# Attention in a hybrid block: exps over two score banks, accumulator copied one step later, maxima split on POOL, rotation from PSUM, first half head by four banks

## The reference, cut to what matters

```
q, k, v = x @ Wq + bq, x @ Wk + bk, x @ Wv + bv      # 16 heads of width 16
q, k = rope(q), rope(k)       # x1*cos - x2*sin, x1*sin + x2*cos
scores = q @ k.T / sqrt(16)   # 4096 x 4096 per head
out = softmax(scores) @ v @ Wo + bo
```

## Time and profile before

| what | value |
|---|---|
| median of 3 runs | 3953.17 us (3945.92 to 3953.18) |
| profiled execution | 3957.6 us, its span 3955.0 us |
| granted clock of PE over the span | 0.953 |
| PE busy | 3614.0 us (91%) |
| DVE busy | 3493.7 us (88%) |
| ACT busy | 2576.7 us (65%) |
| POOL busy | 624.6 us (16%) |
| rotation stage | about 741 to 875 us |
| waiting for the first head's rows | 879.6 to 911.3 us |
| first half head, maxima alone | 912 to 988.6 us |
| steps of attention | about 1001 to 3819 us |
| after attention | 3820 us to the end |

### The profile page before, as it was taken

One profiled execution on the slowest core, in us unless ns is written; L12 is line 12 of the kernel. 1 busy time (PEld: TensorE's weight loads), 2 busy tenths in 40 slices (PEclk: granted clock), 3 DMA queues, 4 the chain that ended last, 5 costly groups with the idle time before them and its releaser, 6 DMA issues. The chain is left out here.

```text
span 3955.0 us, 68507 instructions
## 1 busy us (share of the span) xinstructions
PE 3614.0 (91%) x18757; PEld 1001.7 (25%) x18784; DVE 3493.7 (88%) x5278; ACT 2576.7 (65%) x4673; POOL 624.6 (16%) x436
## 2 busy tenths in 40 slices
PE   5788888857999999999999999999999999999988
PEld 2122222421222222222222222222222222222234
DVE  5999997777999998999999999999999998999815
ACT  5444443550677777777777777777777777777764
POOL 2789894370000000000000000000000000000020
PEclk9899999975899999999999999999999999999999
DMA  1000000341100101010001101000100100010011
GB/s 58 0 1 1 0 0 0 88 99 17 25 13 18 27 3 27 3 27 3 28 12 19 27 3 27 3 27 3 27 19 12 27 3 27 3 27 3 3 53 43
DMA packets 49365, 79.44 MB, mean 20 GB/s; under 512 B 12400, under 2 KB 39536, under 8 KB 44912
## 3 DMA queue, kind: packets, MB, share of 16 engines
q1 hardware_dynamic: 48496, 73.99, 8.2%
q10 hardware_dynamic: 512, 1.05, 0.2%
HBM read 53.37 MB, written 21.23 MB: 19 GB/s over the span
## 5 line engine op out<-in xcount | busy, mean ns | idle before, releaser
L1285 DVE TENSOR_REDUCE part_max<-max_scores 128x1 f32<-128x512 f32 x4096 | 2629.8, 686 | 202.2 <-PE max_scores L1166 154.2
L1267 ACT ACTIVATE prob<-scores 128x512 f32<-128x512 f32 x4096 | 2108.6, 604 | 700.0 <-PE scores L1202 700.0
L1202 PE MATMUL scores<-q_rows,k_rows 99*128 99x512 bf16 x4096 | 1095.6, 387 | 37.2 <-ACT prob L1267 28.4
L1214 PE MATMUL acc<-prob,v_ones 128*32 128x512 f32 x8192 | 1112.7, 616 | 0.0
L1163 PE MATMUL max_scores<-k_twin,q_twin 64*128 64x512 bf16 x2048 | 817.8, 400 | 72.6 <-DMA k_twin<-qk_parts 54.7
L1166 PE MATMUL max_scores<-k_rows,q_rows 64*128 64x512 bf16 x2048 | 818.3, 400 | 20.6 <-DVE part_max L1285 19.6
L1163 PEld LDWEIGHTS max_scores<-k_twin,q_twin 64*128 64x128 bf16 x2048 | 190.1, 93 | 1371.0 <-DVE part_max L1285 1268.1
L1202 PEld LDWEIGHTS scores<-q_rows,k_rows 99*128 99x128 bf16 x4096 | 321.9, 98 | 575.8 <-ACT prob L1267 308.8
L1139 POOL COPY v_ones<-v_all 128x512 f32 (+1 forms) x16 | 9.7, 612 | 2600.6 <-PE acc L1214 2600.5
L512 ACT ACTIVATE decay<-delta,a_scale 128x1024 f32<-128x1024 f32 (+1 forms) x128 | 143.1, 1118 | 300.2 <-DVE scan_state L559 300.2
L597 POOL TENSOR_TENSOR scan_hc<-scan_state,c_rep 128x1024 f32<-128x1024 f32 x128 | 301.8, 2358 | 0.7 <-issue 0.6
(11 more groups left out here) (119 smaller groups left out, 1393.1 us busy)
## 6 DMA issues: line engine op xcount, KB each, us to landing
qk_parts<-roped_parts SPq DMA_DIRECT2D x64, 192.0 KB, 2.9
q_rows<-qk_parts SPq DMA_DIRECT2D x192, 64.0 KB
k_rows<-qk_parts SPq DMA_DIRECT2D x180, 64.0 KB
q_twin<-qk_parts SPq DMA_DIRECT2D x128, 64.0 KB
x_res<-in_x SPq DMA_DIRECT2D x4, 1024.0 KB, 8.8
rope_trig<-in_trig SPq DMA_DIRECT2D x4, 1024.0 KB, 9.0
att_t<-acc_sb SPq DMA_DIRECT2D x128, 32.0 KB
att_all<-att_t SPq DMA_DIRECT2D x8, 512.0 KB, 7.6
```

The costliest lines, as they stand in the source:

```text
L1202: nc.tensor.matmul(sc[:, n % SB, :], k_rows[0:KM, par, kt * P:(kt + 1) * P], q_rows[0:KM, par, q0:q0 + CH], start=True, stop=True).then_in ...
L1214: last = nc.tensor.matmul(acc[32 * i:32 * i + VW, :], v_ones[:, par, kt, :], prob[:, t % PBUF, i * CH:(i + 1) * CH], start=(kt == 0), stop ...
L1267: nc.scalar.activation(prob[:, t % PBUF, j * CH:(j + 1) * CH], sc[:, n % SB, :], ACT.Exp, scale=SCALE).then_inc(exp_done, 1)
L1285: nc.vector.tensor_reduce(part_max[:, t, c:c + 1], mx[:, unit_bank(h, half, u), :], AXX, ALU.max).then_inc(max_read, 1)
```

## The change

Five edits, all in the attention part:

1. One exp instruction covers two score banks (1024 columns) instead of one, so there are two per step. It waits for both score matmuls, and sets both banks free at its end.
2. `acc` is copied behind the exps of the step after (`t == 1` and `t == NKT + 1`).
3. DVE only reduces the maxima to one per query; the four operations that cut it into parts stand on POOL. The partial maxima have a buffer per half head.
4. The rotation multiplies with the sine first, straight from PSUM, and ACT then copies the product crosswise (SBUF to SBUF); the cosine term is written back to PSUM in place; DVE adds the two. The sum leaves POOL, and the low part moves from DVE to POOL. PE may write a bank again once the sum is formed (`roped_ready`).
5. The first half head uses all eight PSUM banks: four max units go to four banks, and one DVE reduction covers the 2048 columns. `qk_parts` is laid out so that a DMA fetches 16 rows instead of 8 (20 DMAs per head), and the first max unit awaits only 16 DMAs: the rows that it uses, and of q only the first half of the queries. The rest is awaited before the second half head's units.

```diff
-        sc = ctx.enter_context(nc.psum_tensor("scores", [P, SB, CH], F32))
-        acc = ctx.enter_context(nc.psum_tensor("acc", [P, CH], F32))
-        mx = ctx.enter_context(nc.psum_tensor("max_scores", [P, MB, CH], F32))
+        banks = ctx.enter_context(nc.psum_tensor("att_banks", [P, 8, CH], F32))
+        sc, acc, mx = banks[:, 0:SB, :], banks[:, SB, :], banks[:, SB + 1:SB + 1 + MB, :]
...
@@ attention, scalar
-                        for j in range(4):
+                        for j in range(0, 4, 2):
                             n = 4 * t + j
-                            act.wait_ge(s_ready, h * (4 * STEPS) + n + 1)
-                            nc.scalar.activation(prob[:, t % PBUF, j * CH:(j + 1) * CH], sc[:, n % SB, :], ACT.Exp,
-                                                 scale=SCALE).then_inc(exp_done, 1)
-                        if t == 0 and not first:
+                            act.wait_ge(s_ready, h * (4 * STEPS) + n + 2)
+                            nc.scalar.activation(prob[:, t % PBUF, j * CH:(j + 2) * CH].rearrange(
+                                "p (b q) -> p b q", q=CH), sc[:, n % SB:n % SB + 2, :], ACT.Exp,
+                                                 scale=SCALE).then_inc(exp_done, 2)
+                        if t == 1 and not first:
                             copy_block(h - 1, 1)
-                        if t == NKT:
+                        if t == NKT + 1:
                             copy_block(h, 0)
...
@@ attention, gpsimd
+                def split_max(h, half):
+
+                    b, cols = 2 * h + half, slice(half * QT, (half + 1) * QT)
+                    wait_apart(pool, low_ready, b + 1, pool_passed)
+                    nc.gpsimd.tensor_copy(neg_parts[:, 0, cols], neg_max[:]).then_inc(split_step, 1)
+                    wait_apart(pool, split_step, b * 3 + 1, pool_passed)
+                    nc.gpsimd.tensor_tensor(neg_rest[:], neg_max[:], neg_parts[:, 0, cols],
+                                            ALU.subtract).then_inc(split_step, 1)
...
                     for par in range(2):
+                        split_max(2 * pair + par, 1)
+                        split_max(2 * pair + par + 1, 0)
 
                         pool.wait_ge(pv_done, (2 * pair + par + 1) * STEPS)
                         copy_v(2 * pair + 2 + par, par)
...
@@ attention, loads and first half head
-                for s in range(2):
-                    r = base + n * DK + s * DK // 2
-                    eng.dma_start(rows[r:r + DK // 2, par, :],
-                                  mem.qk_parts[which, part, s, bass.ds(h * (DK // 2), DK // 2), :]
-                                  ).then_inc(rows_loaded, 16)
+                if n >= skip:
+                    r = base + n * DK
+                    eng.dma_start(rows[r:r + DK, par, cols],
+                                  mem.qk_parts[which, part, bass.ds(h * (DK // 2), DK // 2), :, cols].rearrange(
+                                      "r s t -> (r s) t")).then_inc(done, 16)
...
+                pe.wait_ge(first_loaded, FIRST_LOAD)
                 for u in range(MAXU):
-                    max_unit(0, 0, 0, u)
+                    t, c, g = u // NC, u % NC, u // WIDE
+                    q, out = slice(t * P, (t + 1) * P), wide_banks(g)[:, u % WIDE, :]
+                    if u % WIDE == 0 and g >= 2:
+                        pe.wait_ge(first_read, g - 1)
...
+                pe.wait_ge(rest_loaded, REST_LOAD)
+                pe.wait_ge(first_read, MAXU // WIDE)
...
+                for g in range(MAXU // WIDE):
+                    dve.wait_ge(first_ready, (g + 1) * WIDE)
+                    t, m = g // (NC // WIDE), g % (NC // WIDE)
+                    nc.vector.tensor_reduce(part_max[:, 0, t, m:m + 1], wide_banks(g), mybir.AxisListType.XY,
+                                            ALU.max).then_inc(first_read, 1)
...
@@ attention_project, vector
+                    dve.wait_ge(qk_ready, g + 1)
+                    if later(g - NU + 1):
+                        dve.wait_ge(swap_ready, g - NU + 1)
+                    nc.vector.scalar_tensor_tensor(cross[:, n], qb[:, n], b_qk[:, a, h:h + 1],
+                                                   trig[:, 1, bass.ts(i, CH)], ALU.add, ALU.mult).then_inc(cross_ready, 1)
+                    nc.vector.scalar_tensor_tensor(qb[:, n], qb[:, n], b_qk[:, a, h:h + 1],
+                                                   trig[:, 0, bass.ts(i, CH)], ALU.add, ALU.mult).then_inc(own_ready, 1)
+
+                def add_cross(g, n):
+
+                    dve.wait_ge(own_ready, g + 1)
+                    dve.wait_ge(swap_ready, g + 1)
+                    if later(g - NU + 1):
+                        dve.wait_ge(rest_ready, g - NU + 1)
+                    nc.vector.tensor_tensor(roped[:, n], qb[:, n], swapped[:, n], ALU.add).then_inc(roped_ready, 1)
```

More of the change, by code:

```diff
@@ L801, in attention_project @@
         (loaded, trig_here, std_ready, rstd_ready, xn_ready, t_ready, xnt_ready, v_ready, v_read, qk_ready,
-         swap_ready, terms, roped_ready, hi_ready, rest_ready, mid_ready, lo_ready, stats_done) = make_sems(
-            nc, ctx, "ap", "loaded trighere std rstd xn t xnt v vread qk swap terms roped hi rest mid lo stats")
+         cross_ready, swap_ready, own_ready, roped_ready, hi_ready, rest_ready, mid_ready, lo_ready, stats_done) = make_sems(
+            nc, ctx, "ap", "loaded trighere std rstd xn t xnt v vread qk cross swap own roped hi rest mid lo stats")
         stored = make_sems(nc, ctx, "ap", "stored0 stored1 stored2 stored3")
@@ L864, in pair @@
                                 copy_turned(i + 1, 1 - b)
-                            act.wait_ge(qk_ready, g + 1)
-                            if later(g - NU + 1):
-                                act.wait_ge(terms, g - NU + 1)
-                            nc.scalar.activation(swapped[0:HP, n], qb[HP:P, n], ACT.Copy)
-                            nc.scalar.activation(swapped[HP:P, n], qb[0:HP, n], ACT.Copy).then_inc(swap_ready, 1)
+                            swap(g, n)
                             if later(g):
@@ L890, in what_hi_leaves, with low @@
                                             ALU.subtract).then_inc(rest_ready, 1)
+                def low(g, n):
+                    pool.wait_ge(mid_ready, g + 1)
+                    nc.gpsimd.tensor_tensor(parts[:, n, 2], rest[:, n], parts[:, n, 1],
+                                            ALU.subtract).then_inc(lo_ready, 1)
                 def chunk(i, first, last_chunk):
@@ L894, in chunk @@
                         g = i * NU + n
[L896 to L900 removed]
+                        what_hi_leaves(g, n)
                         if later(g):
[L902 removed]
+                            low(g - 1, (n - 1) % NU)
                 ends_apart(pool, NC, chunk)
[L905 removed]
+                low(NC * NU - 1, NU - 1)
             @block.vector
@@ L958, in _ @@
                 ends_apart(dve, NC // 2, pair)
-                low(NC * NU - 2, NU - 2)
-                low(NC * NU - 1, NU - 1)
+                add_cross(NC * NU - 1, NU - 1)
             @block.tensor
@@ L1050, in turned, with load_rows, load_even_blocks @@
             return mx[:, bank, :].bitcast(BF16)[0:NPART * NT, 0:P]
-        def load_rows(eng, rows, base, which, slots, h, par):
+        def load_rows(eng, rows, base, which, slots, h, par, done, skip=0, cols=slice(0, S)):
             for n, part in enumerate(slots):
-                for s in range(2):
-                    r = base + n * DK + s * DK // 2
-                    eng.dma_start(rows[r:r + DK // 2, par, :],
-                                  mem.qk_parts[which, part, s, bass.ds(h * (DK // 2), DK // 2), :]
-                                  ).then_inc(rows_loaded, 16)
-        def load_even_blocks(eng, h, par):
-            for n, part in enumerate(K_TWIN):
-                for s in range(2):
-                    r = LANE + n * DK + s * DK // 2
-                    blocks = mem.qk_parts[1, part, s, bass.ds(h * (DK // 2), DK // 2), :].rearrange(
-                        "r (b o t) -> r b o t", o=2, t=CH)
-                    eng.dma_start(k_twin[r:r + DK // 2, par, :, :], blocks[:, :, 0, :]).then_inc(rows_loaded, 16)
+                if n >= skip:
[3 more added lines that the diff above has]
+                                      "r s t -> (r s) t")).then_inc(done, 16)
+        def load_even_blocks(eng, h, par, done):
+            for n, part in enumerate(K_TWIN):
+                r = LANE + n * DK
+                blocks = mem.qk_parts[1, part, bass.ds(h * (DK // 2), DK // 2), :, :].rearrange(
+                    "r s (b o t) -> (r s) b o t", o=2, t=CH)
+                eng.dma_start(k_twin[r:r + DK, par, :, :], blocks[:, :, 0, :]).then_inc(done, 16)
         def heads(eng, body):
@@ L1170, in turn_max @@
                 def turn_max(h, half, last=False):
-                    pe.wait_ge(max_read, turn_slot(h, half, last) - MB + 1)
```

(3 more changed lines are left out.)

143 lines of the change are left out of this document (76 added, 67 removed).

## The result

The changed kernel takes **3809.26 us** (median of 4 runs, 3804.19 to 3811.22) against 3949.61 for the kernel before (4 runs, 3945.92 to 3953.18): ratio 0.9643, interval 0.9626 to 0.9659. The forecast was 3792, the range 3760 to 3850. The profiled executions took 3804.19 and 3957.6, their spans are 3802.1 and 3955.0; the 152.9 us between the spans stand against the 161 of the sum.

The account below looks back on a forecast made before the run. PE was taken to set the 2.61 us step, with time to gain in longer steps and the stages before; 57 + 27 + 28 + 0 + 19 + 5 + 25 = 161 us off gave a median of 3792 us, range 3760 to 3850.

Parts of the forecast that it names:

- Copies, 57: Accumulator copies inside the steps: copied one step later, nothing waits; 57 us for 31 copies, ends 60 and 42.
- Clock, 27: PE's clock in the steps: its falls go if the copy's stall causes them; 27 us, ends 30 and nothing.
- Split, 28: Splits of the maxima, moved to POOL: 28 us from the split's step and the transposition's, 30 times; ends 43 and 10.
- Loads, 19: Wait before attention's first matmul: fewer bytes awaited and 16 rows using twice the DMA engines gain 19 us, otherwise 11.
- First half head, 5: Maxima before the steps: one DVE reduction over four banks saves fixed cost; 5 us, between 0 and 8.
- Rotation, 25: Rotation stage before the steps: less DVE work and less DVE idling; 25 us, between 8 and 38.
- Wide exps, none: 1024-column exps: no gain where PE sets the steps, nothing in the last half head; ends gain 5, loss 10.
- Loop jumps keep their 25: Six jumps back of the head loop: each step 4.2 us over a plain one, 25 us in all, unchanged.
- rival that loads and code meet: Loop jumps: row fetches filling all DMA engines delay code, 5 us more at six jumps, 3822 us; chance 0.06.
- end with all good terms: Whole kernel: rotation 38, split 40, loads 21, first half head 8, giving 3765 us; chance 0.10.
- POOL comes late: POOL's split stalls PE 0.9 to 2 us at 30 transpositions and clock falls return: 3820 to 3880 us; chance 0.11.
- exps set the step: All 1024 steps: a wide exp repeating beyond 1.11 us lengthens each; at 1.30, 3987 us; chance 0.03.

Follow-up runs that it names:

- E1: The changed kernel with the accumulator's copy put back behind the exps of step 0 and step 32: 3882.56 us, ratio 0.9831.
- E2: The kernel before, with only the accumulator's copy moved one step later: 3870.25 us, ratio 0.9803.
- E12: The changed kernel with 26 more casts on POOL ahead of its split of the maxima: 3894.88 us, ratio 0.9861.
- E6: The changed kernel with each load of rows cut into two of eight rows, from the same memory: 3804.08 us, ratio 0.9631.
- E8: The changed kernel with the rotation stage of the kernel before, parts stored as in the changed kernel: 3825.23 us, ratio 0.9691.
- E4: The changed kernel with the four further operations of the split moved from POOL back to DVE: 3830.55 us, ratio 0.9702.
- E7: The changed kernel with 16 more casts on POOL ahead of its split of the maxima: 3829.79 us, ratio 0.9711.
- E5: The changed kernel with the loads of the next head's rows issued four steps later, past the loop's jump: 3789.55 us, ratio 0.9594.
- E3: The changed kernel with exps of 512 columns over one bank each, four to a step: 3821.12 us, ratio 0.968.

## Why the prediction was right

Forecast and outcome, by its own steps:

- **Copies, 57:** right. They cost nothing now, E1 brings 1.9 us each back, E2 takes them away alone.
- **Clock, 27:** right in sum ("rest" 27.4 to 1.8, 18 falls to none). The cause is told too simply. It is no property of the copy: E12 makes 14 falls with a late split, and E1, with the copies back, only 7. By the rule of the Trainium skill ("TensorE: Matmul & The Clock Gate", on its second failure mode) the cycling through banks would have kept the clock swinging; at 1.00 with the same cycling the trace speaks against it here. Away from the jumps the falls stood behind waits of PE of about 1.9 us.
- **Split, 28:** 26.4 came, from other steps than named. The split's own stall went almost wholly (0.2 was to stay, 0.08 did), and at the transposition nothing was given back: 0.47 before and now.
- **Loads, 19:** 18.7 (the wait went from 31.65 to 12.95). E6 shows the cause of 10.5 of them, half the engines with eight rows. The other 8.2 are left for the rows that the first matmul no longer awaits, which no run tests by itself. The rule of the Trainium skill ("DMA: Bandwidth & Descriptors", on why a DMA raises its semaphore by 16) agrees: a share of 0.49 with eight rows and of 1.01 with sixteen.
- **First half head, 5:** from first matmul to first weighing 98.07 went to 93.24, 4.8. A reduction of 2048 columns repeats each 39.66 / 18 = 2.20 us, as said. No run undoes this part alone.
- **Rotation, 25:** 27.3 in the trace, of which E8 ties 25 to it. From 745 us to the start of the loads DVE is busy for 89.2 us instead of 107.9, 18.7 less where 21.5 were named; the rest is idle time of DVE that went.
- **Wide exps, none: the step that failed.** It has "which comes to about 2.0. Nothing." The round of the banks in the last half head is 4.25 us for two steps, 2.12 a step and not 2.0, so 63.56 us instead of 58.74: 4.8 lost (the last two of the 31 steps have weighings alone). The stated end, a loss of 10, held it.
- **Loop jumps keep their 25:** the step at the jump was 26.6 us over in all and is 30.2 now. The rival that loads and code meet had the right mechanism, at about a quarter of its price: 7.7 us by E6 instead of 30. That size is uncertain, since "jumps" goes from 35.8 to 46.7 among E4, E7, E8, E12 and the changed kernel, which all have the same loads and wide exps; E5 and E6 lie below all of them.

In the spans, 8 us are missing of the 161: 5 in the last two half heads, by the exps; 2 at the transposition, and some 3 at the jumps and the start; less 2 that the stages ahead of the steps gave more, which is the scatter of 2.6 that E8 and E1 show. That the medians differ by 140.3 and not 152.9 has another cause: the profiled execution of before, 3957.6, is slower than all runs shown (8.0 over their median), that of after is the fastest of its four (5.1 under it). The forecast took 4.4 off for the first and could not know the second. So of the 17 us between 3792 and 3809.26 some 8 are missing terms and 9.5 are the choice of executions; all lay inside the range. That the end with all good terms was put at 3765 is a small slip: its four terms add up to 30 us more, 3762.

The other rivals: the clock goes on falling away from the jumps, no; POOL comes late, no, with 1.7 us to spare (E7), and it would have cost as much as was said (E12: 86 us at 1.9 us late); exps set the step, no, a pair takes 1.94 us.

## What to carry to other kernels

When one engine sets the pace, move the work that makes it wait behind work that it doesn't need yet, and check how late it may come: here 1.7 us of slack cost nothing, and 1.9 us beyond it more than half the gain. At each jump back of the loop PE stood for 3.2 to 4.0 us here, DVE and ACT stood with it, and loads beside the jump made it longer. Count such jumps (here 39 us for six) before tuning what lies between, and write the loop out or keep transfers off it.

## What the runs showed that was not expected

- A wait of PE of about 1.9 us brings PE's clock down only sometimes: 7 falls with 24 copies away from the jumps (E1), 14 with 30 late splits (E12), and none behind stalls of 0.95 us or waits of 0.53 (E2, E4, E7). With stalls of 0.95 and 1.85 in each half head, and narrow exps, it was 18 with 24 copies. What decides in the single case is not shown.
- Twice as many DMA engines carried the first load at 126 instead of 85 GB/s, and the head's loads in the steps at no higher rate, yet PE stood longer at the jump.
- The width of ACT's instructions changed what the jumps cost by 20 us (E3), where DVE stood up to 4.00 us with no releaser in the trace, some 10 us behind the jump. Why stays open. ACT has 4673 instructions with narrow exps instead of 2625, but that alone does not do it: E2 has narrow exps with loads of eight rows, and its jumps cost 35.4 us.
